# A two-layer post-norm decoder on one core: the stages outside the cross attentions split into two chains of 224 columns

## What is computed

```
x = LN(x + linear_attention(x))                      # Wq, Wk, Wv, Wo, causal sums
x = LN(x + xattn_block(x, ctx))                      # see below
x = LN(x + ffn_fp6(x))                               # x and weight quantized in blocks of 32
x = LN(x + memory_block(x))                          # conv, gates, a scan, bucket memory, then an MLP
x = LN(x + cross_attention(x, ctx))                  # 16 heads of 8, context 1500
x = LN(x + mixture_of_experts(x))                    # top 2 of 8, plus shared experts
...
def xattn_block(x, ctx):
    x = LN(x)*g+b;  x = x + mha(x, x, causal=True)   # self attention and MLP 1 (gelu)
    x = LN(x)*g+b;  return x + mha(x, ctx)           # cross attention 1 and MLP 2 (gelu)
def mha(x, y): 
    o = softmax(q(LN x) k(LN y)) v(LN y); x_out = x + o @ li1; return x_out + gelu(LN(x_out) @ li2) @ li3
```

## Time and profile before

| | |
|---|---|
| median of 3 runs | 749.22 us (748.0 to 750.85) |
| the profiled execution | 749.95 us, its span 748.2 us |
| TensorE busy | 666.2 us (89%), weight loads 464.6 us beside it |
| VectorE busy | 500.9 us (67%) |
| ScalarE busy | 330.1 us (44%) |
| GpSimd busy | 340.5 us (46%) |
| filler matmuls (line 198) | 749 records, 101.6 us |

### The profile page before, as it was taken

The page is one execution under the profiler, slowest core; times in us unless marked ns, Lnnn a source line. Parts: engine busy times, 40 slices in busy tenths (PEclk is TensorE's granted clock), DMA queues, the critical chain, the costliest instruction groups (busy, mean ns, idle before and its releaser), DMA issues.

```text
span 748.2 us, 19799 instructions
## 1 busy us (share of the span) xinstructions
PE 666.2 (89%) x8821; PEld 464.6 (62%) x8821; DVE 500.9 (67%) x779; ACT 330.1 (44%) x449; POOL 340.5 (46%) x256
## 2 busy tenths in 40 slices
PE   9868888869999999999877777789999999999987
PEld 5535754547777777777644453466777777776752
DVE  3365832778888888886324464288889888888532
ACT  2123444243555466464242303425664664564441
POOL 1070435044876976764200144008667766845300
PEclk9998999998999999999999988999999999999998
DMA  9500003000000000000030000000000000000000
GB/s 255 199 0 1 4 1 125 1 1 2 2 3 2 2 3 2 2 3 2 2 136 4 1 0 1 0 2 1 3 2 2 3 2 2 3 2 2 2 1 12
DMA packets 3360, 14.81 MB, mean 20 GB/s; under 512 B 356, under 2 KB 484, under 8 KB 3276
## 3 DMA queue, kind: packets, MB, share of 16 engines
q1 hardware_dynamic: 3276, 13.56, 5.6%
HBM read 13.33 MB, written 0.23 MB: 18 GB/s over the span
## 4 chain that ended last, share of the span: by engine, by line
PE 67%; DVE 14%; ACT 9%; POOL 5%; issue 4%; DMA 1%; POOLq 0%; DVEq 0%; ACTq 0%
PE psum L840 16%; PE psum L749 8%; PE psum L798 5%; PE psum L198 5%; PE psum L791 5%; PE psum L793 4%; DVE scratch L918 3%; POOL scratch L903 2%; PE psum L213 2%; PE psum L206 2%; PE psum L740 1%; PE psum L731 1%; ACT scratch L865 1%; PE psum L755 1%; PE psum L599 1%
## 5 line engine op out<-in xcount | busy, mean ns | idle before, releaser
L903 POOL TENSOR_TENSOR scratch<-scratch 125x896 bf16<-125x896 f32 x136 | 232.3, 1718 | 150.4 <-ACT scratch L893 149.7
L893 ACT ACTIVATE scratch<-psum 125x896 f32<-125x896 f32 x192 | 173.9, 917 | 201.5 <-PE psum L840 199.7
L918 DVE TENSOR_REDUCE scratch<-psum 128x1 f32<-128x500 f32 x336 | 210.7, 672 | 17.6 <-PE psum L749 8.9
L840 PE MATMUL psum<-scratch 128*125 128x448 bf16 (+1 forms) x768 | 178.1, 357 | 4.0 <-issue 3.7
L749 PE MATMUL psum<-scratch 128*128 128x500 bf16 x336 | 127.1, 378 | 12.2 <-DVE scratch L918 7.3
L840 PEld LDWEIGHTS psum<-scratch 128*125 128x125 bf16 (+1 forms) x768 | 97.9, 137 | 34.8 <-issue 4.5
L791 PE MATMUL psum<-tok,scratch 125*128 125x65 bf16 x1344 | 109.4, 196 | 1.8 <-DVE kT L963 1.8
L793 PE MATMUL psum<-tok,scratch 125*128 125x64 bf16 x1344 | 108.8, 193 | 0.0
L791 PEld LDWEIGHTS psum<-tok,scratch 125*128 125x128 bf16 x1344 | 95.9, 97 | 14.0 <-issue 2.8
L198 PE MATMUL psum<-w_second 128*128 128x256 bf16 x749 | 101.6, 278 | 0.0
L793 PEld LDWEIGHTS psum<-tok,scratch 125*128 125x128 bf16 x1344 | 90.7, 99 | 14.6 <-issue 0.3
(11 more groups left out here) (307 smaller groups left out, 775.8 us busy)
## 6 DMA issues: line engine op xcount, KB each, us to landing
raw<-ctx_dram SPq DMA_DIRECT2D x4, 672.0 KB
w_third<-fifth_dram SPq DMA_DIRECT2D x3, 636.0 KB, 5.3
w_fourth<-fourth_dram SPq DMA_DIRECT2D x3, 566.5 KB, 6.6
w_third<-third_dram SPq DMA_DIRECT2D x2, 844.0 KB, 22.3
w_third<-third_dram SPq DMA_DIRECT2D x2, 843.5 KB, 20.4
w_first<-first_dram SPq DMA_DIRECT2D x1, 996.0 KB, 5.0
w_second<-second_dram SPq DMA_DIRECT2D x1, 834.0 KB, 6.8
w_third<-fifth_dram SPq DMA_DIRECT2D x1, 636.5 KB, 7.4
```

Of the source, the lines that this page charges most:

```text
L840: mm = nc.tensor.matmul(bank(S + f, HALF, CP), lhs[0:rows, CP * c:CP * c + CP], rhs[0:rows, HALF * f:HALF * f + HALF], start=(rows == 128) ...
L893: nc.scalar.activation(CR["p"][0:CP, n % RING, :].rearrange("p (f n) -> p f n", f=2), psum[0:CP, S:S + 2, 0:HALF], ACT.Exp).then_inc(self. ...
L903: ops.tensor_tensor(CR["pl"][0:CP, n % RING, :], CR["p"][0:CP, n % RING, :], p_high(n % RING), ALU.subtract).then_inc(done, 1)
L918: nc.vector.tensor_reduce(mxp[:, r, t:t + 1], bank(B, TB), X_AXIS, ALU.max).then_inc(self.aux_freed, 1)
```

## The change

The columns of every stage outside the cross attentions are dealt with in two halves of 224 (batches 0 to 3 and 4 to 7). Each half has PSUM banks of its own: 0 and 1 for centring, 6 and 7 for mean matmuls and output projections, 2 and 3 for MLP projections. Norms, MLPs, output projections, fp6 output, memory output, the last sum and the store each issue twice as many instructions of half the width. Besides:

- WARM goes from 6 to 2, and the fillers ahead of the output projections of attention 0 (20) and cross attention 1 (16) are gone.
- The MLP projections of batches that are finished are issued ahead of the last batches' outputs.
- The context's sums and squares move beside attention 0.
- The quantization of the fp6 weights moves from cross attention 1 to MLP 2's wait for "down".
- `dec` is made by Exp and a reciprocal inside cross attention 1, so that GpSimd can make `carry` after MLP 2; GpSimd also splits the first tokens of cross attention 2 in between.
- Queries are made in two halves with the token transposes between them.

```diff
-WARM, WARM2 = 6, 8
+WARM, WARM2 = 2, 8
...
+        HALVES = (slice(0, N // 2), slice(N // 2, N))
+        CEN, VAR, PROJ = (0, 1), (6, 7), (2, 3)
+        UP = ((2, 3, 4, 5), (6, 7, 2, 3))
...
+        def ln_pe(pe, k, x, ready):
+
             if k == 0:
                 pe.wait_ge(loaded["second"], 16)
+            for p, cols in enumerate(parts_of(k)):
+                pe.wait_ge(*ready[p])
+                nc.tensor.matmul(cen(k, p), par("center"), x[:, cols], start=True, stop=True).then_inc(ln_cen, 1)
             if k:
                 keep_warm(WARM)
             ln_mean(pe, k)
...
+            for p, cols in enumerate(parts_of(k)):
+                act.wait_ge(ln_var, 2 * k + p + 1)
+                nc.scalar.activation(lv[:, cols], var(k, p), ACT.Ln,
+                                     bias=col("eps", 0 if x is None else 1)).then_inc(ln_log, 1)
+                act.wait_ge(ln_log, 2 * k + p + 1)
+                nc.scalar.activation(rstd[:, cols], lv[:, cols], ACT.Exp, scale=-0.5).then_inc(ln_rstd, 1)
...
-            keep_warm(20, 7)
-            pe.wait_ge(a0_act.sem, a0_act.count(f"o{PAIRS-1}"))
             pe.wait_ge(loaded["second"], 16)
+            for p, cols in enumerate(HALVES):
+                pe.wait_ge(a0_act.sem, a0_act.count(f"o{2 * p + 1}"))
...
+        CONTEXT_BESIDE = {0: [], 1: [(context_sum, 0)], 2: [(context_sum, 1)], 3: [(context_sum, 2), (context_var, 0)]}
...
+            mlp1.proj_pe(pe, "a1", 0, [HALVES[0]], a1_act.sem, a1_act.count(f"o{PAIRS-3}"))
+            mlp1.proj_pe(pe, "a1", 1, [slice(N // 2, 336)], a1_act.sem, a1_act.count(f"o{PAIRS-2}"))
             outputs(PAIRS - 1)
...
+                if projection is not None:
+                    done = self.index("O", 0, BATCH - 2)
+                    pe.wait_ge(self.probs, CHUNKS * BATCH)
+                    projection(0, [HALVES[0]], self.aux_freed, self.freed(done))
+                    projection(1, [slice(N // 2, N - SEQ)], self.aux_freed, self.freed(done))
                 for unit in self.last:
-                    keep_warm(4, 2)
+                    keep_warm(4, 2 if projection is None else 4)
                     self.pe_unit(pe, *unit)
-                keep_warm(WARM_G, 2)
+                if projection is None:
+                    keep_warm(WARM_G, 2)
...
-                    if self is cross1 and n == 3:
-                        fp6_weights_dve(dve)
...
+            mlp2.run_dve(dve, "a2", xa, fp6_weights_dve, x1)
...
+        def carry_pool(pool):
+            pool.wait_ge(decay_set, 1)
+            pool.wait_ge(outer, 2)
...
             mem_pool_early(pool)
+            pool.wait_ge(mlp2.dve.sem, mlp2.dve.count("xo1"))
+            cross2.split_tokens(pool, 0, 0)
+            pool.wait_ge(cross2.tok_set, 1)
+            carry_pool(pool)
+            pool.wait_ge(fp6_dve.sem, fp6_dve.count("sum1"))
+            cross2.split_tokens(pool, 0, 1)
```

More of the change, by code:

```diff
@@ L597, in updown_pe @@
[L597 to L605 removed]
+                self.pe = sig(tag + "_pe", ["proj0", "proj1"] * proj + ["up00", "up10", "up20", "up30", "up01", "up11",
+                                                                        "up21", "up31", "down0", "down1"])
@@ new lines, in __init__, with proj_pe @@
+                self.act = sig(tag + "_act", ["up00", "up10", "up20", "up30", "up01", "up11", "up21", "up31"])
+                self.dve = sig(tag + "_dve", ["xo0", "xo1", "h0", "h1", "sum", "res0", "res1"])
+            def proj_pe(self, pe, w, p, groups, ready, value):
+                pe.wait_ge(ready, value)
+                at = parts_of(self.k)[p]
+                for cols in groups:
+                    for j in range(4):
+                        mm = nc.tensor.matmul(psum[:, PROJ[p], cols.start - at.start:cols.stop - at.start],
+                                              par(w + "_li1", 128 * j, 128 * j + 128), oT[:, j, cols],
+                                              start=(j == 0), stop=(j == 3))
+                    if cols.stop == at.stop:
+                        mm.then_inc(*self.pe.done(f"proj{p}"))
@@ new lines, in run_dve @@
+            def run_dve(self, dve, w, x, meanwhile=None, outer_of=None):
+                norm_dve(dve, self.k, xn, self.dve, "h", w + "_ln3_g", w + "_ln3_b")
+                dve.wait_ge(self.dve.sem, self.dve.count("h1"))
+                nc.vector.tensor_tensor(t1[:, 0:N], xo[:, 0:N], x[:, 0:N], ALU.add).then_inc(*self.dve.done("sum"))
+                if meanwhile is not None:
+                    meanwhile(dve)
+                for p, cols in enumerate(parts_of(self.k)):
+                    dve.wait_ge(self.pe.sem, self.pe.count(f"down{p}"))
+                    dve.wait_ge(self.dve.sem, self.dve.count("sum"))
+                    nc.vector.scalar_tensor_tensor(t1[:, cols], cen(self.k, p), col(w + "_li3_b"), t1[:, cols], ALU.add,
+                                                   ALU.add).then_inc(*self.dve.done(f"res{p}"))
+                    if outer_of is not None:
+                        dve.wait_ge(self.dve.sem, self.dve.count(f"res{p}"))
+                        nc.vector.tensor_tensor(t1[:, cols], t1[:, cols], outer_of[:, cols], ALU.add).then_inc(outer, 1)
@@ L1696, in _ @@
-            dve.wait_ge(ln_b.sem, ln_b.count("xn_g"))
-            nc.vector.tensor_scalar(xn[:, 0:N], t2[:, 0:N], col("a2_lnx_b"), None, ALU.add).then_inc(*ln_b.done("xn"))
-            cross1.tokens_dve(dve)
-            cross1.run_dve(dve)
-            mlp2.run_dve(dve, "a2", xa, None)
-            dve.wait_ge(mlp2.dve.sem, mlp2.dve.count("res"))
-            nc.vector.tensor_tensor(t1[:, 0:N], t1[:, 0:N], x1[:, 0:N], ALU.add).then_inc(outer, 1)
-            norm_dve(dve, 7, x2, ln_c.done("x2"))
+            for p in PARTS:
+                mlp1.first_dve(dve, "a1", xa, p)
```

465 lines of the change are left out of this document (252 added, 213 removed).

## The result

The new kernel takes 705.37 us (703.84 to 707.01, four runs) against 749.41 of the kernel before beside it: a ratio of 0.941 (0.938 to 0.945). The profiled execution took 707.01 us with a span of 705.2, 43.0 less than the span before.

A forecast was written before the change was run, and what follows sets the result against it. Outside the two cross attentions no engine was the bound, but a chain of dependent steps. The savings, less item 12's loss, summed to 36.0 us: 749.2 - 36.0 = 713, range 704 to 725.

The forecast's parts named there:

- case A: Whole kernel: everything goes as forecast, 33 to 39 us saved; chance 0.57.
- Rival B: x quantization: item 12 does not happen, load late enough or quantization over; 5.4 us more saved, 708; chance 0.15.
- item 12: x quantization: contention with GpSimd's cast, subtraction and carry loses 3.4, clock fall about 2.0, halves give 0.6; net loss 4.8 us.
- item 15: Output projection, norm 12, router, last sum and norm 13: saves 2.95 us.
- The half chain: Norms in halves: 3.5 us without gain, 3.95 with it, saving 1.15 or 1.25 us each.
- Item 7: Cross attention 1: the weights' quantization leaves, first batch nears attention 2's 24.8 us; saves 7.7 us.
- Item 8: End of cross attention 1 and projection 2: earlier projections cost 1.9, 16 fillers (1.85) go; saves 2.2 us.
- Item 9: MLP 2's wait for "down": the weights' quantization takes 3.8 us there, ends about 0.9 before down1, no cost.
- Items 3 and 4: Norm 1 saves 2.9 us (halves, GpSimd's centring mostly moved ahead); norm 2 and the queries save 4.35 us.
- Item 13: Norm 8 saves 1.15, norm 9 1.05, the freed convolution 2.8, its clock fall 2.0; net 7.0 us.
- Rival E: All chains: with fewer fillers TensorE is granted 1.2 GHz, costing 46 us against 36, 759; chance 0.02.
- items 1 and 8: Item 1: end of the first attention without 20 fillers saves 2.3 us. Item 8: saves 2.2 us.

The follow-up runs named there:

- the release: The new kernel with GpSimd's first split and the carry tile released by the end of the x quantization in place of the load: 704.45 us.

## Why the prediction was right

The direction and the main mechanism, chains of halves, were right. The size is less of a merit: 705.4 lies in the range of 704 to 725, but 7.6 under 713 and beyond case A, which had 33 to 39 us saved where 44 were. Rival B, at 708 and with a chance of 0.15, came true in its contention (0.8 for 3.4) and not in its clock. The range reached below 707 for a norm 2 or an MLP better than counted, and neither came: 4.0 for 4.35, 2.55 for 2.6. What filled it were item 12 (4.3 too low) and item 15 (2.3, most of it a fall of the clock in the execution before), so the foot of the range was met by luck. Of the signs, norm 2's centring (46.2 and 46.95), the first batch (23.9 us) and the convolution (2.12 us) came; the quantization of 11 us did not. And the clock did fall in a chain, at 424 us in norm 10 with MLP 3, which the prediction had named as a sign of being wrong.

- **The half chain** (items 2 to 6, 10, 11, 13 to 15). 3.15 us without gain for the 3.5 worked out, 3.8 with gain for 3.95. c1 follows c0 by 0.7 us, and the second Ln waits for nothing. Ln of the first half begins 1.06 us after c1, where the terms gave 1.3. The run with whole ScalarE operations shows that the overlap on ScalarE makes it.
- **Item 12** is the step that failed, by its time and not by its mechanism: its 3.4 us of contention were 0.8. The load landed 10.1 us after MLP 2's second result (357.54 to 367.63) in place of 8.9, which is 5.75 us after the quantization's start and not 4.3. So little was left of the quantization that the carry, behind cast and subtraction, began when its last operation had been running for 0.8 us. Forced into it, the carry costs what was predicted (11.0 us); where the load landed at 4.3 to 4.7 it did so by itself (11.5). The prediction knew of the case (rival B, 0.15) and should have given it more: one row gave the landing time, and in the runs it lies between 8.9 and 10.4 us.
- **The clock behind item 12** fell all the same, at 372, behind an idle of 1.14 us, as item 12 said. Its price stands in item 13. The measured -0.5 is 0.8 of contention less 0.3 that the halves of the output step gave (0.6 forecast).
- **Item 7**: 8.7 for 7.7. I had taken cross attention 2 as the measure (24.8); batch 0 of cross attention 1 now takes 23.9.
- **Item 8**: 1.35 for 2.2. Of it the split is 0.25; the rest comes with the 16 fillers and the halves, which no run takes apart. The cost ahead (1.9) was right; the gain behind was put too high. The terms that the item names (1.85, 2.6 and -1.9) also add to 2.6 and not to 2.2; the 0.375 by which c1 follows c0 would make the difference, but the item does not say so.
- **Item 9**: nothing, as said, with 0.46 us to spare for 0.9.
- **Items 3 and 4**: right in sum (7.05 for 7.25). The context's move weighs more in them than was said: with halves its undoing costs 6.8, where about 3.6 had been expected of it.
- **Item 13**: 5.9 for 7.0. The convolution gave its 2.8; norm 8 paid for the low clock of 372: from its c0 to the convolution it is 8.1 us, and 7.0 where the clock stays up (carry behind the quantization). The 2.0 that the item took for a clock fall behind the convolution came back in part, at 400 us.
- **Item 15**: 5.25 for 2.95, of which 1.5 is the clock of the execution before; of the rest norm 13 and the store have 0.45.
- **Rival E** had its mechanism right and its condition wrong: the fillers do hold the clock, and in the new kernel's profile the ten that are left in a norm are enough from 28 to 372 us. Two other runs' profiles have a fall at 74 us with these fillers.
- **The clock as a whole** is what the sum left out. Behind attention 0 it is low for 36 us of the execution before and for 15 of the new one. Three falls of together 13.7 us cost 5.0 in the new kernel, so an estimate from these rows is that about 8 of the 43 us are falls that did not come. The prediction counted two of those falls, and some of these come and go from one execution to the next.

What stays open is why the clock falls in one execution and not in another. The new kernel idles 3.31 us before 401 and the clock is at 0.50 behind it; with the release the same 3.31 us end at 399.97 and the clock stays at 1.00. Not tested are the 20 and 16 fillers ahead of the output projections by themselves (items 1 and 8), and the move of `dec`.

## What to carry to other kernels

A chain of short steps on three engines gains from halves if the engine with the most steps in it can work on one half while the others have the other; here a norm whose ScalarE work stayed whole gained nothing. Divide that engine's work first, and look at the second half's start to size it. A large operation of a side engine should be released by the end of the stage that it can block, not by the load that happens to come before: about a microsecond in the landing of a load decided 3 us here, and it did so unasked in three experiments that were about something else. So look in every experiment's trace for side effects of this kind before giving its whole difference to the edit. Fillers that hide behind a wait cost at most 0.2 us a norm here; count the clock's falls in several executions before giving one to an edit.

## What the runs showed of the hardware

- A tensor_scalar with a single SBUF input is blocked by a GpSimd tensor_tensor until that ends or shortly after: 2.52 us for 0.17 (0.03 us after), 2.80 for 0.34 (0.13 after). In three profiles a VectorE operation that begins 0.5 us after the carry takes 3.54 us for 0.69; in the new kernel's, one that had begun 0.8 us before it ends in 1.27. GpSimd pays too, less: the carry takes 3.17 us behind the quantization and 3.50 where it begins beside an operation of it.
- TensorE's clock fell behind different idles in different executions (372, 400 and 424 us in one, 74, 418 and 442 in that with the carry's release), beside one in attention 0 that all thirteen profiles have. The three of the new kernel cost 5.0 us together (59.6 for 54.6 from norm 8 to norm 11, against the profile with more fillers). The new kernel's four executions differ by 3.2 us.
